# Second edge layer: relation lookups and score reductions for four steps at once, each product between two additions of sums

## What is computed

```python
Q = (enh @ Wq + bq).reshape(N, H, D)          # H = 4 heads, D = 64
K = (enh @ Wk + bk).reshape(N, H, D)
V = (enh @ Wv + bv).reshape(N, H, D)
rel = rel_w[edge_relations]
mod_k = K[src] + 0.2 * rel[:, None, :]
scores = jnp.einsum('ehd,ehd->eh', Q[dst], mod_k) / D ** 0.5
seg_max = jax.ops.segment_max(scores, dst, num_segments=N)
ex = jnp.exp(scores - seg_max[dst])
denom = jax.ops.segment_sum(ex, dst, num_segments=N)
w = ex / denom[dst]
agg = jax.ops.segment_sum(w[:, :, None] * V[src], dst, num_segments=N)
```

## Time and profile before

| | us |
|---|---|
| median of 3 runs | 2019.4 (2018.72 to 2021.09) |
| the profiled execution's own time | 2017.31 |
| its span, first to last instruction | 2015.6 |
| DVE busy | 1477.4 (73%) |
| PE busy | 1381.4 (69%) |
| ACT busy | 1100.7 (55%) |
| POOL busy | 1079.6 (54%) |

### The profile page before, as it was taken

How to read it: one execution, slowest core, us unless ns; L and a number is a source line. 1 busy time by engine, 2 the same in 40 slices (tenths; PEclk the granted TensorE clock), 3 DMA queues, 4 the chain that set the end, 5 groups by cost and what they waited for, 6 DMA issues and landing times. The chain is left out here.

```text
span 2015.6 us, 29940 instructions
## 1 busy us (share of the span) xinstructions
PE 1381.4 (69%) x6938; PEld 955.9 (47%) x6938; DVE 1477.4 (73%) x3722; ACT 1100.7 (55%) x4270; POOL 1079.6 (54%) x1124
## 2 busy tenths in 40 slices
PE   5346576676576319997866787788878777665086
PEld 4234444444354217775444555555555554354064
DVE  5568787887787863445869999999999998776143
ACT  2256666766666313322441888888888888232033
POOL 1377777777774300000527777777777775100555
PEclk9667777777777559998987988988888888866599
DMA  5744444444442019000458767766667664225465
GB/s 126 192 127 131 132 124 125 137 123 136 129 123 58 3 42 325 2 0 6 146 194 252 204 196 204 205 201 200 197 199 205 195 195 142 61 66 118 164 190 141
DMA packets 141115, 287.87 MB, mean 143 GB/s; under 512 B 25507, under 2 KB 66977, under 8 KB 140821
## 3 DMA queue, kind: packets, MB, share of 16 engines
q0 software_dynamic: 58192, 175.85, 30.2%
q1 hardware_dynamic: 82758, 110.13, 18.6%
HBM read 241.17 MB, written 48.86 MB: 144 GB/s over the span
## 5 line engine op out<-in xcount | busy, mean ns | idle before, releaser
L769 POOL DMA_INDIRECT e_rows<-h_rows,src_col x416 | 429.6, 1033 | 127.0 <-issue 124.5
L1214 POOL DMA_INDIRECT e_rows<-kv_rows,src_col x320 | 307.7, 962 | 99.7 <-issue 58.9
L930 ACT ACTIVATE e_rows<-e_rows 128x32 f32<-128x32 f32 x1664 | 357.7, 305 | 0.8
L999 PE MATMUL e_sum<-e_rows,e_of_dst 128*128 128x264 f32 x832 | 293.5, 506 | 77.8 <-DVE e_rows L866 71.1
L1469 ACT ACTIVATE e_rows<-e_rows 128x64 f32<-128x64 f32 x1168 | 292.7, 335 | 0.3
L1547 PE MATMUL e_query<-q,e_to_dst 128*128 x1248 | 215.5, 309 | 90.4 <-DVE e_rows L1282 68.0
L999 PEld LDWEIGHTS e_sum<-e_rows,e_of_dst 128*128 128x128 f32 x832 | 196.0, 251 | 128.8 <-DVE e_rows L866 78.3
L1588 PE MATMUL e_sum<-e_rows,e_of_dst 128*128 128x260 f32 x640 | 205.5, 447 | 3.9 <-DVE acc L1370 3.4
L1547 PEld LDWEIGHTS e_query<-q,e_to_dst 128*128 128x128 bf16 x1248 | 124.7, 104 | 146.2 <-issue 104.8
L1370 DVE TENSOR_TENSOR acc<-acc,e_sum 128x260 f32 x299 | 125.8, 421 | 54.8 <-PE e_sum L1588 20.7
L1588 PEld LDWEIGHTS e_sum<-e_rows,e_of_dst 128*128 128x128 f32 x640 | 122.8, 216 | 31.7 <-DVE acc L1370 13.8
(11 more groups left out here) (402 smaller groups left out, 2911.8 us busy)
## 6 DMA issues: line engine op xcount, KB each, us to landing
sorted_rows<-zeros SPq DMA_DIRECT2D x1, 14560.0 KB
rows<-sorted_rows SPq DMA_DIRECT2D x56, 260.0 KB, 2.9
e_rel<-step_rel SPq DMA_DIRECT2D x26, 512.0 KB, 4.1
e_to_dst<-step_rel SPq DMA_DIRECT2D x52, 256.0 KB, 4.1
e_rows<-h_rows,src_col POOLq DMA_INDIRECT x416, 2.9
e_to_typ<-step_typ SPq DMA_DIRECT2D x52, 128.0 KB
e_rows<-kv_rows,src_col POOLq DMA_INDIRECT x320, 3.8
kv_rows<-kv SPq DMA_DIRECT2D x5, 768.0 KB, 3.5
```

What stands on the lines that cost most here:

```text
L769: pool.indirect_dma_start(out=g[t // BATCH % R][:, t % BATCH, :], out_offset=None, in_=k.h_rows[:, :], in_offset=bass.IndirectOffsetOnAxis ...
L930: ins = act.activation(x, x, ACT.Copy, scale=row[:, D + h:D + h + 1])
L999: pe.matmul(psm[t % NB], of_dst[q][:, s % GROUP, :], g[m % R][:, s, :], start=True, stop=True).then_inc(summed, 1)
L1214: pool.indirect_dma_start(out=rows_at(t, 1)[:, 0, :], out_offset=None, in_=k.kv_rows[:, :], in_offset=bass.IndirectOffsetOnAxis(ap=k.src_c ...
```

## The change

`score_add` and `score_reduce` now take four steps, a quad, `QUAD = 4`, over 1024 elements in a partition; `score_multiply` still takes a pair. `ps_r` holds four steps a buffer. PE's `look` is split: `look_relations` makes 12 matmuls for a quad every second slot, ahead of the slot's two sums, and `look` makes the six matmuls of the queries behind them. On DVE a slot now starts with a quad's addition (even slots) or a quad's reduction (odd slots from 3 on; the last quad of a lot in slot 0), and the pair's product stands between the additions of the slot's two sums. The load of the window numbers stands at the slot's start. A quad's addition waits for the rows of all four of its steps.

```diff
-        def score_add(m, q):
-            t = m * LONG + q * QP
-            keys = rows_at(t, QP)[:, :, 0:D].rearrange("p s (h f) -> p s h f", h=H)
-            at, count = pair_at(t)
-            v.wait_ge(related, m * PAIRS2 + (q + 1))
-            v.wait_ge(rows_in[at], count)
-            c.inc(v.tensor_tensor(keys, keys, ps_r[q % 2].unsqueeze(2).to_broadcast([P, QP, H, F]), ALU.add))
-            with_relation[m * PAIRS2 + q] = c.count
+        def score_add(m, u):
+            t = m * LONG + u * QUAD
+            keys = rows_at(t, QUAD)[:, :, 0:D].rearrange("p s (h f) -> p s h f", h=H)
+            v.wait_ge(related, m * QUADS + (u + 1))
+            for at, count in (pair_at(t), pair_at(t + QP)):
+                v.wait_ge(rows_in[at], count)
+            c.inc(v.tensor_tensor(keys, keys, ps_r[u % 2].unsqueeze(2).to_broadcast([P, QUAD, H, F]), ALU.add))
+            with_relation[m * QUADS + u] = c.count
...
-        def score_reduce(m, q):
-            at = slice(q * QP, (q + 1) * QP)
-            v.wait_ge(look_used, m * PAIRS2 + (q + 1))
-            keys = rows_at(m * LONG + q * QP, QP)[:, :, 0:D]
+        def score_reduce(m, u):
+            at = slice(u * QUAD, (u + 1) * QUAD)
+            v.wait_ge(look_used, m * PAIRS2 + 2 * (u + 1))
+            keys = rows_at(m * LONG + u * QUAD, QUAD)[:, :, 0:D]
...
-                if more:
-                    score_add(m + 1, q)
-                if q == 1:
+                if first >= 0 and first % 8 == 0:
+                    w = load_windows(first, 8)
+                if more and q % 2 == 0:
+                    score_add(m + 1, q // 2)
+                if q == 0:
+                    score_reduce(m, QUADS - 1)
+                    if m:
+                        hot(m - 1, 7)
+                elif q == 1:
...
+                if more and q % 2 and q > 1:
+                    score_reduce(m + 1, q // 2 - 1)
+                if q == 3:
+                    made = reduce_contexts(made)
+                elif first == m * LONG and m:
+                    v.wait_ge(k.dve_steps, c.count)
+                    rescale(m, w[0])
+                if q % 4 == 1 and (m + 1) * LONG // CHUNK + q // 4 + 1 < CHUNKS:
+                    masks((m + 1) * LONG // CHUNK + q // 4 + 1)
+                add(first, w)
...
                 if more:
                     score_multiply(m + 1, q)
...
-                add(first, w)
...
                 add(first + 1, w)
...
+        def look_relations(m, u):
+            h, quad = m * LONG // CHUNK + u // 2, m * QUADS + u
+            typ = slice(h % 2 * F, (h % 2 + 1) * F)
+            if u % 2 == 0:
+                pe.wait_ge(masks_ready, h + 1)
+            if quad >= 2:
+                pe.wait_ge(k.dve_steps, with_relation[quad - 2])
+            for t in range(QUAD):
...
+        for q in range(PAIRS2 + 1):
+            look_ahead(0, q, True)
+            look_ahead(0, q, False)
         for m in range(LOTS2):
             for q in range(PAIRS2):
                 first = m * LONG + 2 * q - FIRST_SUM
-                if q + 1 < PAIRS2:
-                    if m + 1 < LOTS2:
-                        look(m + 1, q + 1)
-                elif m + 2 < LOTS2:
-                    look(m + 2, 0)
+                look_ahead(m + 1, q + 1, True)
                 if q == 4:
                     turn_probabilities(m)
                 add_up(first)
                 add_up(first + 1)
                 if q == 0:
                     turn_scores(m)
-                elif q == 1:
+                look_ahead(m + 1, q + 1, False)
+                if q == 1:
                     turn_tips(m)
                 elif q == 2:
                     turn_context(m)
```

More of the change, by code:

```diff
@@ L1029, in edges_second @@
     PAIRS2 = LONG // QP
+    QUAD = 2 * QP
+    QUADS = LONG // QUAD
     CHUNK = 8
@@ L1118, in edges_second @@
     ps_q = [ps(f"query{b}", [P, QP, D]) for b in two]
-    ps_r = [ps(f"relation{b}", [P, BANK])[:, 0:QP * F].rearrange("p (s f) -> p s f", f=F) for b in two]
+    ps_r = [ps(f"relation{b}", [P, BANK])[:, 0:QUAD * F].rearrange("p (s f) -> p s f", f=F) for b in two]
     filled = sem("filled")
@@ L1383, in _ @@
         for q in range(PAIRS2):
-            score_add(0, q)
-            if q:
-                score_reduce(0, q - 1)
+            if q % 2 == 0:
+                score_add(0, q // 2)
+            elif q > 1:
+                score_reduce(0, q // 2 - 1)
             score_multiply(0, q)
@@ L1406, in _ @@
                     factors(m)
-                elif q == 5:
-                    hot(m, 1)
-                elif q == 9:
-                    hot(m, 3)
-                elif q == 13:
-                    hot(m, 5)
-                if q == 0:
-                    score_reduce(m, PAIRS2 - 1)
-                elif more:
-                    score_reduce(m + 1, q - 1)
-                if q == 0 and m:
-                    hot(m - 1, 7)
-                elif q == 1:
+                elif q in (5, 9, 13):
+                    hot(m, q // 4 * 2 - 1)
+                if more and q % 2 and q > 1:
[9 more added lines that the diff above has]
+                if q == 1:
                     ends_of_steps(m, made)
@@ L1423, in _ @@
                 elif q == 3:
-                    made = reduce_contexts(made)
-                if q % 4 == 1 and (m + 1) * LONG // CHUNK + q // 4 + 1 < CHUNKS:
-                    masks((m + 1) * LONG // CHUNK + q // 4 + 1)
+                    v.wait_ge(k.dve_steps, made)
+                    made = scans(m, ini[:, 0:1], ini[:, 1:2])
                 if more:
                     score_multiply(m + 1, q)
-                if first >= 0 and first % 8 == 0:
-                    w = load_windows(first, 8)
                 if q == 2 and m:
@@ L1433, in _ @@
                 elif q == 3:
-                    v.wait_ge(k.dve_steps, made)
-                    made = scans(m, ini[:, 0:1], ini[:, 1:2])
-                if first == m * LONG and m:
-                    v.wait_ge(k.dve_steps, c.count)
-                    rescale(m, w[0])
-                add(first, w)
+                    made = maxima(made)
+                add(first + 1, w)
                 if q == 2 and m:
@@ L1442, in _ @@
                 elif q == 3:
-                    made = maxima(made)
-                add(first + 1, w)
-                if q == 3:
                     differences(made)
@@ L1527, in _ @@
         load_windows = windows(pe, "pe_win")
+        def look_relations(m, u):
[6 more added lines that the diff above has]
+            for t in range(QUAD):
+                s = u % 2 * QUAD + t
+                for j in range(3):
+                    mm = pe.matmul(ps_r[u % 2][:, t, :], to_typ[h // 2 % 2][typ, s * P:(s + 1) * P],
+                                   k.by_typ[typ, j, :], start=(j == 0), stop=(j == 2))
+            mm.then_inc(related, 1)
         def look(m, q):
             h, pair = m * LONG // CHUNK + q // CHUNK_PAIRS, m * PAIRS2 + q
-            typ = slice(h % 2 * F, (h % 2 + 1) * F)
-            if q % CHUNK_PAIRS == 0:
-                pe.wait_ge(masks_ready, h + 1)
             w = load_windows(m * LONG + q * QP, QP)
-            if pair >= 2:
-                pe.wait_ge(k.dve_steps, with_relation[pair - 2])
-            for t in range(QP):
-                s = q % CHUNK_PAIRS * QP + t
-                for j in range(3):
-                    mm = pe.matmul(ps_r[q % 2][:, t, :], to_typ[h // 2 % 2][typ, s * P:(s + 1) * P],
-                                   k.by_typ[typ, j, :], start=(j == 0), stop=(j == 2))
-            mm.then_inc(related, 1)
             wait(pe, look_used, pair - 1)
@@ L1551, in turn_scores @@
         def turn_scores(m):
-            pe.wait_ge(scored, (m + 1) * PAIRS2)
+            pe.wait_ge(scored, (m + 1) * QUADS)
             wait(pe, prob_in_rows, m)
@@ L1589, in add_up, with look_ahead @@
                       start=True, stop=True).then_inc(summed, 1)
-        for q in range(PAIRS2):
-            look(0, q)
-        look(1, 0)
+        def look_ahead(m, q, relations):
+            if q == PAIRS2:
+                m, q = m + 1, 0
+            if m >= LOTS2:
+                return
+            if not relations:
+                look(m, q)
+            elif q % 2 == 0:
+                look_relations(m, q // 2)
+        for q in range(PAIRS2 + 1):
+            look_ahead(0, q, True)
+            look_ahead(0, q, False)
         for m in range(LOTS2):
```

4 lines of the change are left out of this document (2 added, 2 removed).

## The result

The changed kernel takes 2031.5 us (median of 7 runs, 2024.78 to 2037.29), the kernel before 2021.09 (7 runs, 2018.72 to 2027.37). The ratio is 1.0045, interval 1.0023 to 1.0067. It is slower by 0.45%, where 1998.7 was forecast. The profiled execution took 2031.5 us, its span is 2029.8. Of the 14.2 us between the two spans, 12.8 lie in the second edge layer, whose first gather starts 1.4 us later (1043.26 instead of 1041.88); ten lots from 1135.25 on last 51.51 us each instead of 50.41. The profiled execution of the kernel before was a short one, 2017.31 against a median of 2021.09, so up to 0.3 us of these 1.1 a lot (3.8 us over 13 lots) can be scatter.

What follows compares the result with a forecast made beforehand. DVE bounds it, just (92% busy); afterwards a loop of 2.3 + 0.26 + 21.1 + 4.0 + 20.9 = 48.6 us a lot instead of 50.4, over 11.5 lots: 2019.4 - 20.7 = 1998.7 us. Range 1982 to 2017, own range 1989 to 2011.

Steps and rivals of the forecast that it cites:

- Fixed part of 0.07 us: DVE's fixed cost per instruction; 8 additions and 8 reductions fewer a lot save 1.1 us (0.8 to 2.4).
- Product between additions: On DVE, a product between a slot's two additions removes the wait for its own addition: 1.05 us a lot saved.
- PE's sums ahead of queries: On PE, sums go before queries that wait for a product, freeing most of DVE's 1.15 us a lot; 0.9 counted.
- Waits for rows: DVE waits for DMA ahead of L1277, above all at a lot's slot 0, some 8 to 20 us in all.
- Step 4 of the loop: Landing of the last of four gathered rows before DVE's addition in the next slot 0: taken as 4.0 us.
- the loop that I forecast: Slot 6 to next slot 6 through DVE, POOL's gathers and row landing: 48.6 us a lot, against 50.4 before.
- step 5: Slots 0 to 5, to the next slot 6: 20.9 us, including 0.6 (0 to 2) of waits in slots 3 and 4.
- Step 3: POOL, from its addition of step 1 to the gather made at step 15, never waits: 21.1 us for 15 gathers.
- the sign of being wrong that I named: POOL's gathers between slots 6 and 0 take more than 21.1 us, for instance because DVE's denser stream slows them.
- Ends: First and last lots: about 2 us lost at the start and won back, last lot 0; taken as 0 (-1 to +3).
- slower, 2028: Rival: four rows land late, 6.4 us after the gather, loop 51.0 us, deciding from a landing of 5.8; chance 0.08.
- DVE alone: Rival: rows land in time and DVE alone sets the pace, 3.1 us a lot saved, 1983 us; chance 0.17.

Runs made afterwards that it cites:

- the order alone: Kernel before with only the new order on DVE and PE, additions and reductions of two steps: 2009.66 against 2017.08 us, ratio 0.9959; other groups 0.996, 0.9945.
- the version with additions of two: Changed kernel with relations added for two steps, reductions still of four, against the kernel before: 2008.49 us, ratio 0.9935; other groups 1.0011, 1.002.

## Why the prediction was wrong, point by point

- **Fixed part of 0.07 us.** Right where the next instruction follows at once: L1277 starts 1.13 before it (1376.06 to 1377.19), busy 1.22. But I counted sixteen such savings. Worked out from the starts of ten lots, eight additions of four take 9.4 us instead of 9.6, eight reductions 9.2 instead of 9.5, and all of DVE's work 46.5 instead of 46.8: 0.3 us a lot, not 1.1. The register load at the slot's start (0.13 more at 1364.35 to 1364.82) and the rescale behind a longer addition take the rest. The Trainium skill's term of 150 cycles ("VectorE: DVE Perf Modes", the section on the fixed extra latency) fits the busy figures of 0.68 and 1.22 again; the saving didn't follow it.
- **Product between additions.** Right on DVE (12.2 us of waits to none), wrong in what it is worth. So are PE's sums ahead of queries. Together 0.5 us a lot instead of 1.95, since DVE then waits for POOL instead (in the order alone in slots 0, 8 and 11, 0.8, 0.3 and 0.9 us a lot).
- **Waits for rows.** The kind was forecast (L1277 waits for DMA, 8 to 20 us; measured 22.5), their place was half right: slots 0 and 12 were named; the wait stands in slot 12 in ten lots of ten, in slot 0 once.
- **Step 4 of the loop, "Landing ... I take 4.0", is the step that failed for the rows.** I took a median for one gather that stands beside label loads in every lot. It was not a median over 416 gathers either, as the prediction says: the trace gives the landing of 76. And I closed the loop over slot 0; there the changed kernel has 5.4 to 5.8 us from the last gather to the addition, the row lands in 3.7, and nothing waits. Closed over slot 12 in the measured lot: 2.62 from slot 6's start (1364.82) to POOL's addition of step 1, 9.68 to the gather at 1377.12, 6.95 to the addition at 1384.07, 11.30 for slots 12 to 15 and 20.56 for slots 0 to 5: 51.11 us, to the next slot 6 at 1415.93. The mean lot has 51.51. The landing there was 6.4 in the mean, not 4.0.
- **But this step is only 1.0 of the 2.9 us by which the lot missed 48.6.** Without label loads, the rows in time, the loop that I forecast closes over slot 0 at 50.6 us (ten lots from slot 6 to slot 6): 2.65 to POOL's addition of step 1 (forecast 2.56), 21.5 to the last gather (21.1), 4.2 to the addition (4.0) and 22.3 for slots 0 to 5 (20.9). So the other term that was mis-sized is **step 5**: I gave waits in slots 0 to 5 0.6 us, and that kernel has 1.6 us of waits for PE there. In the changed kernel step 5 looks fair, 21.2, but its slots 0 to 5 follow a wait for rows in slot 12, in which the other engines may catch up (no run shows it); in the order alone and in the version with additions of two they take 21.7 and 21.5, hardly less than the 21.8 before.
- **Step 3**, 21.1 us, is one lot. The ten lots of the kernel before take 21.6 in the mean, those of the changed kernel 21.9: the sign of being wrong that I named (more than 21.1) came, but since POOL's additions wait for DVE's, not since a denser DVE stream slows the gathers.
- **The range.** From landing 3.5 to 5 and waits of 0 to 1.5 the forecast's own terms give lots of 47.5 to 50.5 us, so 1986 to 2021, and not 1989 to 2011.
- **Ends.** Forecast 0 (-1 to +3). By lot 2 the loss is 3.2 us (1138.46 against 1135.25): 1.4 stand ahead of the first gather, 0.7 lie between it and the first addition (1056.89 instead of 1054.84), 1.9 in the first lot, and 0.7 come back in the second. The first addition doesn't wait for its four rows; it follows a mask without a pause. With ten lots of 1.1 us, 10.9, this is the 14.2 us between the spans.
- **The rivals.** The one that came true is "slower, 2028", with its mechanism (rows that land late, deciding from 5.8 us on), though I priced it at 0.08 on the ground that the median is 3.8 and three additions ever waited before. The second was true and no evidence: before, that row came 0.17 us ahead of its use, 5.8 us after its gather in the mean of ten lots, just the landing from which this rival decides. That its price of 2028 lies near the 2031.5 measured is in part luck: it has all rows late over slot 0 and slots 0 to 5 at 20.9. "DVE alone" (1983) is refuted: even with the rows in time the lot is 50.5, with 1.8 us of waits for POOL and 2.0 for PE in it.

## What to carry to other kernels

When a change makes an instruction wait for more transfers, look up for each place in the loop the very transfer that would come last, when it landed and when it would now be used; a median over all transfers says nothing of the one that stands beside another engine's loads each lap. Merge what waits for nothing (the reductions) apart from what waits for rows, and time them apart. A saving on the fullest engine counts only in the part of the loop where no other engine runs without a pause: find such a run (11.88 us here) before adding savings up. Read a term of a loop from several laps: one lap gave 21.1 where ten gave 21.6.

## What the runs showed of the hardware

- A gather of 128 rows lands 5.1 us after its start if a broadcast load of labels is issued within about 2 us of it, up to 6.9, and after some 3.7 us otherwise; the mean DMA share from 1 to 4 us behind its start is then 0.82 instead of 0.66. Loads moved by one pair of steps move the late landing with them, and without loads the latest row of a lot lands in 3.5 us instead of 6.4.
- POOL's pitch of gathers and additions is the same to 0.03 us (11.88 to 11.91 for eight gathers and three additions) in kernels whose DVE streams differ, in the laps in which it doesn't wait.
- The ratio of two kernels differed by up to 0.8% between groups of runs (0.9935 and 1.002). A comparison holds for the conditions in which it was made.
